# A graph attention layer on one core: aligned parts of V, rows added by GpSimd, late stores, and a first stage with two reductions on GpSimd

## The reference

```python
h = jnp.maximum(_layernorm(x, axis=-1), 0.0)              # x: 4096 x 128, float32
# in the layer, with node_features = h:
h = node_features @ W.T + b_W                              # W: 128 x 128
a1, a2 = (a_vec[:D_OUT], a_vec[D_OUT:])
e = (h @ a1)[:, None] + (h @ a2)[None, :] + b_a[0]         # 4096 x 4096
e = jnp.where(e > 0, e, 0.2 * e)
scores = jnp.where(adjacency_matrix > 0, e, -9e15)         # adjacency: int32, 4096 x 4096
attention = jax.nn.softmax(scores, axis=1)
return x + attention @ h
```

## Time and profile before

| | |
|---|---|
| median of 3 runs | 204.99 us (204.95 to 205.09) |
| profiled execution, its own time | 206.4 us |
| its span, first to last instruction | 204.8 us |
| PE busy | 200.0 us (98%), 3183 matmul instructions |
| PEld busy | 193.5 us (94%) |
| DVE busy | 183.8 us (90%) |
| ACT busy | 142.1 us (69%) |
| POOL busy | 43.7 us (21%) |
| DMA | 75.66 MB, mean 369 GB/s |

### The profile page before, as it was taken

One profiled execution on the slowest core, in us unless ns is written; L12 is line 12 of the kernel. 1 busy time (PEld: TensorE's weight loads), 2 busy tenths in 40 slices (PEclk: granted clock), 3 DMA queues, 4 the chain that ended last, 5 costly groups with the idle time before them and its releaser, 6 DMA issues.

```text
span 204.8 us, 7172 instructions
## 1 busy us (share of the span) xinstructions
PE 200.0 (98%) x3183; PEld 193.5 (94%) x3183; DVE 183.8 (90%) x271; ACT 142.1 (69%) x129; POOL 43.7 (21%) x60
## 2 busy tenths in 40 slices
PE   7989999999999999999999999999999999999994
PEld 7558888999999999999999999999999999999993
DVE  4679999899999799997999998979999899889854
ACT  2289977699770777789777756798777767966000
POOL 1000669699996011070000000000000000000000
PEclk9999999999999999999999999999999999999999
DMA  5999999999999999999999999999999999960312
GB/s 180 366 417 415 405 406 429 413 406 369 429 429 414 418 421 421 416 422 416 413 419 424 402 416 427 422 419 426 414 419 403 406 426 418 426 278 14 104 44 64
DMA packets 15968, 75.66 MB, mean 369 GB/s; under 512 B 1600, under 2 KB 5952, under 8 KB 7616
## 3 DMA queue, kind: packets, MB, share of 16 engines
q1 hardware_dynamic: 15792, 75.06, 90.1%
q10 hardware_dynamic: 144, 0.13, 0.3%
HBM read 73.08 MB, written 2.11 MB: 367 GB/s over the span
## 4 chain that ended last, share of the span: by engine, by line
PE 97%; ACT 1%; issue 0%; DVE 0%; POOL 0%; POOLq 0%
PE ps L834 30%; PE ps L832 28%; PE ps L838 28%; PE ps L806 4%; PE ps L796 3%; PE ps L848 2%; ACT L409 1%; PE ps L874 1%; ACT hT L335 0%; PE ps L852 0%; PE ps L857 0%; DVE xT L539 0%; PE ps L851 0%; DVE rg L512 0%; POOL ones L715 0%
## 5 line engine op out<-in xcount | busy, mean ns | idle before, releaser
L832 PE MATMUL ps<-V,w 128*128 128x129 f16 x1024 | 177.2, 220 | 0.0
L834 PE MATMUL ps<-V,w 128*128 128x129 f16 x1024 | 177.2, 223 | 0.0
L838 PE MATMUL ps<-V,w 128*128 128x129 f16 x1024 | 177.2, 219 | 0.0
L377 ACT ACTIVATE mask<-adj_sb 128x2048 bf16<-128x2048 int32 x63 | 119.6, 1914 | 35.2 <-DMA adj_sb<-in_adj_t 32.4
L457 DVE SCALAR_TENSOR_TENSOR w<-g_row,pairs,mask 128x1024 f32<-128x1024 f32 x96 | 117.7, 1285 | 7.4 <-ACT mask L377 5.0
L838 PEld LDWEIGHTS ps<-V,w 128*128 128x128 f16 x1024 | 102.0, 100 | 0.0
L834 PEld LDWEIGHTS ps<-V,w 128*128 128x128 f16 x1024 | 99.7, 97 | 1.0 <-issue 1.0
L832 PEld LDWEIGHTS ps<-V,w 128*128 128x128 f16 x1024 | 99.2, 97 | 1.5 <-ACT H L340 0.7
L457 DVE SCALAR_TENSOR_TENSOR w<-ps,pairs,mask 128x1024 f32<-128x1024 f32 x31 | 37.5, 1268 | 0.7 <-ACT mask L377 0.7
L786 POOL PARTITION_ALL_REDUCE bad<-bad x1 | 0.4, 380 | 111.3 <-DVE bad L530 111.3
L806 PEld LDWEIGHTS ps<-wp,hT 128*128 128x128 f32 x64 | 8.1, 198 | 2.3 <-ACT hT L335 1.7
(11 more groups left out here) (93 smaller groups left out, 64.6 us busy)
## 6 DMA issues: line engine op xcount, KB each, us to landing
adj_sb<-in_adj_t SPq DMA_DIRECT2D x64, 1024.0 KB, 10.5
xT<-in_x_t SPq DMA_DIRECT2D x8, 256.0 KB, 7.4
x_sb<-in_x_p SPq DMA_DIRECT2D x3, 512.0 KB, 10.8
g_row<-g_dram SPq DMA_DIRECT2D x1, 1536.0 KB, 11.5
out<-xT SPq DMA_DIRECT2D x3, 512.0 KB, 11.4
x_sb<-in_x_p SPq DMA_DIRECT2D x2, 256.0 KB, 4.5
out<-xT SPq DMA_DIRECT2D x1, 192.0 KB, 2.1
out<-xT SPq DMA_DIRECT2D x3, 64.0 KB, 1.5
```

What stands on the lines that cost most here:

```text
L377: nc.scalar.activation(mask[:, m % MASKS, :], adj_sb[:, m % HELD, :], ACT.Relu, scale=CONNECTED).then_inc(mask_ready, 1)
L832: nc.tensor.matmul(sums[:, bank, a, :], w16[:, m % SLOTS, col:col + P, 1], V[:, jt, 0:NF], start=(jt == 0 and a == 0), stop=False, skip_gr ...
L834: nc.tensor.matmul(sums[:, bank, a, :], w16[:, m % SLOTS, col:col + P, 1], V[:, jt, NF:2 * NF], start=False, stop=False, skip_group_check= ...
L838: last = nc.tensor.matmul(sums[:, bank, a, :], w16[:, m % SLOTS, col:col + P, 0], V[:, jt, 0:NF], start=False, stop=(jt == NT - 1), skip_g ...
```

## The change

It has five parts.

1. `V` gets rows of 2 x 136 fp16 numbers instead of 258, and each part uses the first 129 of its 136. Each part now begins at a multiple of 16 bytes.
2. The rows of groups 0 to 2 are added by POOL instead of DVE, behind its first check reduction. The three stores of these rows stand behind the last `adj` load in SP's list instead of between the loads.
3. `norm` and b's constant are reduced by POOL with `partition_all_reduce`. ACT squares W itself and sums along its rows, POOL takes the maximum and the root (`pow` with one half). PE loses L852 and L857. DVE waits for `root_ready` later in its list than before.
4. The first tile of the first `adj` pair is loaded by a DMA of its own, ahead of the second tile, and DVE makes its mask in two halves. There are 7 warming matmuls, and the first centring stands ahead of W a.
5. `ENDS` is 3 instead of 4, and the last check stands behind the reciprocal of the last piece.

```diff
@@ V, WARM, ENDS
+    VW = DOUT + 8
-    WARM = 8
+    WARM = 7
-    ENDS = 4
+    ENDS = 3
-        V = sb("V", [P, NT, 2 * NF], F16)
+        V = sb("V", [P, NT, 2, VW], F16)
@@ SP
+                sp.dma_start(adj_sb[:, 0, 0:GC], adj_t[0, :, 0:GC]).then_inc(tile_loaded, 16)
                 load_xt(3)
-                load_adj(0)
+                sp.dma_start(adj_sb[:, 0, GC:2 * GC], adj_t[0, :, GC:2 * GC]).then_inc(adj_loaded[0], 16)
...
-                    if group >= 2 and at == STORE_AT:
-                        store(group - 2, GI * (group - 2), GI * (group - 1))
-                store(NG - 2, GI * (NG - 2), GI * (NG - 1))
+                for r in range(NG - 1):
+                    store(r, GI * r, GI * (r + 1))
@@ ACT
-                    act.wait_ge(norm_ready, 1)
-                    nc.scalar.activation(root[:], norm[:], ACT.Sqrt).then_inc(root_ready, 1)
...
+                nc.scalar.activation(wsq[:], wp[:, 0:DIN], ACT.Square, scale=(1.02 * DIN) ** 0.5,
+                                     accum_out=norm[:, 0:1]).then_inc(squares_ready, 1)
@@ DVE, first stage
-                dve.wait_ge(norm_summed, 1)
-                nc.vector.tensor_reduce(norm[:], ps[:, 4, 0:DOUT], AX_X, ALU.max).then_inc(norm_ready, 1)
                 statistics(1)
-                dve.wait_ge(cc_done, 1)
+                dve.wait_ge(cc_done, 2)
...
-                early_mask()
+                early_mask(1)
+
+                dve.wait_ge(root_ready, 1)
+                step_(nc.vector.tensor_scalar(gg[:, 0:1], root[:], 1e-30, None, ALU.max))
+                nc.vector.reciprocal(gg[:, 1:2], gg[:, 0:1]).then_inc(g_ready, 1)
+                dve.wait_ge(g_ready, 1)
+                step_(nc.vector.tensor_scalar(rstd[:, 2, 0:GI], rstd[:, 1, 0:GI], gg[:, 1:2], None, ALU.mult))
                 pack(0)
                 scale_weights(0)
+                ones_of(0)
...
-                statistics(2, 5, 8)
+                statistics(2, 3, 8)
@@ DVE, later
-                    if past >= 0 and at in ROWS_AT:
-                        add_rows(past, ROWS_AT.index(at))
@@ POOL
+                pool.wait_ge(wp_loaded, 16)
+                nc.gpsimd.tensor_scalar(ba[:, 0:2], wp[:, AV:AV + 2], wp[:, BW:BW + 1], None, ALU.mult).then_inc(cc_done, 1)
+                pool.wait_ge(cc_done, 1)
+                nc.gpsimd.partition_all_reduce(ba[:, 2:4], ba[:, 0:2], P, RADD).then_inc(cc_done, 1)
+                pool.wait_ge(squares_ready, 1)
+                nc.gpsimd.partition_all_reduce(norm[:, 1:2], norm[:, 0:1], P, RMAX).then_inc(norm_ready, 1)
+                pool.wait_ge(norm_ready, 1)
+                nc.gpsimd.tensor_tensor(root[:], norm[:, 1:2], half_col[:], ALU.pow).then_inc(root_ready, 1)
                 deviations(2, 3)
...
+                for r in range(2 * (NG - 1)):
+                    k = slice(GI // 2 * r, GI // 2 * (r + 1))
+                    pool.wait_ge(scaled_rows, r + 1)
+                    nc.gpsimd.tensor_tensor(Z[:, k, :], Z[:, k, :], x_sb[:, k, :], ALU.add).then_inc(rows_added, 1)
@@ PE
-                nc.tensor.matmul(ps[:, 6, 0:2], wp[:, BW:BW + 1].to_broadcast([P, P]), wp[:, AV:AV + 2], start=True,
-                                 stop=True).then_inc(cc_done, 1)
-                pe.wait_ge(squares_ready, 1)
-                nc.tensor.matmul(ps[:, 4, 0:DOUT], ones[:], wsq[:], start=True, stop=True).then_inc(norm_summed, 1)
```

More of the change, by code:

```diff
@@ L15 @@
 RMAX = bass.bass_isa.ReduceOp.max
+RADD = bass.bass_isa.ReduceOp.add
 LN_EPS = 1e-5
@@ L306, in store @@
                 def store(r, first, last):
-                    sp.wait_ge(rows_ready, 2 * r + 2 if r < NG - 1 else r + NG)
+                    if r < NG - 1:
+                        sp.wait_ge(rows_added, 2 * r + 2)
+                    else:
+                        sp.wait_ge(rows_ready, r - NG + 2)
                     sp.dma_start(out_v[:, first:last, :], Z[:, first:last, :]).then_inc(stored, 16)
                 for m in range(4, NM):
-                    group, at = divmod(m, PAIRS)
                     load_adj(m)
@@ L469, in weigh_first, with early_mask @@
                                                    ALU.min).then_inc(w_begun if half == 0 else w_ready, 1)
-                def early_mask():
-                    dve.wait_ge(adj_loaded[0], 16)
-                    nc.vector.tensor_scalar(mask[:, 0, 0:GC], adj_sb[:, 0, 0:GC], CONNECTED, 0.0, ALU.mult,
+                def early_mask(half):
+                    r = slice(half * GC // 2, (half + 1) * GC // 2)
+                    dve.wait_ge(tile_loaded, 16)
+                    nc.vector.tensor_scalar(mask[:, 0, r], adj_sb[:, 0, r], CONNECTED, 0.0, ALU.mult,
                                             ALU.max).then_inc(mask_early, 1)
@@ L489, in inverse_sums @@
                                             ALU.mult).then_inc(rg_ready, 1)
[L491 to L495, removed]
                 def inverse_last(i):
@@ L510, in inverse_last @@
                         nc.vector.tensor_copy(den[:, r], of).then_inc(den_ready, 1)
+                    else:
+                        check_last()
                     dve.wait_ge(rden_ready, NG - 1 + i + 1)
@@ L567, in scores, with ones_of @@
                                             ALU.mult).then_inc(scores_ready, 1)
+                    if part > 0:
+                        ones_of(part)
+                def ones_of(part):
+                    r = slice(*PARTS[part])
                     nc.vector.reciprocal(H[:, r, ONE], rstd[:, 2, r]).then_inc(ones_ready, 1)
@@ L631, in _ @@
                 nc.vector.reciprocal(rstd[:, 1, 0:GI], rstd[:, 0, 0:GI]).then_inc(std_ready, 1)
-                dve.wait_ge(root_ready, 1)
-                step_(nc.vector.tensor_scalar(gg[:, 0:1], root[:], 1e-30, None, ALU.max))
-                nc.vector.reciprocal(gg[:, 1:2], gg[:, 0:1]).then_inc(g_ready, 1)
-                dve.wait_ge(g_ready, 1)
+                statistics(2, 0, 3)
                 dve.wait_ge(std_ready, 2)
-                step_(nc.vector.tensor_scalar(rstd[:, 2, 0:GI], rstd[:, 1, 0:GI], gg[:, 1:2], None, ALU.mult))
-                statistics(2, 0, 3)
                 scores(0)
@@ L642, in _ @@
                 nc.vector.tensor_reduce(tt[:, 0:1], st[:, 0:GI, T], AX_X, ALU.max).then_inc(t_limits, 1)
-                statistics(2, 3, 5)
+                early_mask(0)
                 dve.wait_ge(t_spread, 1)
```

45 lines of the change are left out of this document (23 added, 22 removed).

## The result

The changed kernel has a median of 221.07 us in four runs (218.51 to 224.66) beside 205.04 for the kernel before; the ratio is 1.074 [1.064, 1.084]. The comparison leaves the run of 224.66 out as disturbed; the other three have a median of 220.46. The profiled execution took 218.51 us with a span of 216.9, so 12.1 us of span more than before.

What follows compares the result with a forecast made beforehand. PE was taken as the bound, 3072 matmuls back to back from the first product. Late root +11.7, clock +2.0, alignment -3.6, step 7 +0.3, end +0.3 make +10.7 us on 204.99: 215.7 us, range 200 to 220.5.

Steps and rivals of the forecast that it cites:

- POOL's code: POOL's first stage: each change between plain operations and reductions costs about 9.1 us of issue; root_ready at 25.9 us.
- The first ISA row: POOL, ahead of the first small product: between 0 and 9.1 us, taken at half, 4.6, for little DMA load.
- The 6 us of the page: Skill page's cost for the first call of freshly loaded POOL code; at 6 us each, root_ready 21.1, time 211.
- Clock and the way to the first product: From root_ready: 0.6 for DVE, 0.8 for pack, 2.7 on PE, 2.0 for PE's clock falling while idle.
- Ends 0 and 4: Range in us given for the loss by PE's lower clock around the first product; 2.0 was taken.
- Alignment: PE's product matmuls: aligned V rids L834 of its excess, gain 3.6 us by durations, 2.8 by chain shares.
- an odd multiple of two bytes: Supposed cause of L834's 223 ns median against 220 and 219: where its read of V's low part starts.
- rival B: Product matmuls: L834's excess belongs to the weights, so aligning V brings nothing; 219.3 us, chance 0.12.
- Rows and stores at 0: Row additions moved to POOL and stores moved behind the loads gain nothing, as PE waits for neither; 0 us.
- Step 7: Products, where DVE's lead is narrowest: PE will wait there for about 0.3 us (0 to 1).
- The end: Behind the last matmuls: with ENDS 3, DVE's closing work and checks add 0.3 us (-0.1 to 0.5).
- Rival A: POOL's code change is short or hidden: 201.3 us, chance 0.28; root_ready costs nothing up to 14.1 us.

Runs made afterwards that it cites:

- par_only: The changed kernel with both reductions on POOL, but b's product and the root made by ACT; 202.82 us, ratio 0.988 to the kernel before.
- hidden_reload: The kernel before with one unused partition_all_reduce added at the head of POOL's list; 205.14 us, ratio 1.001.
- pool_norm_only: The kernel before with part 3 of the change alone (norm and b's constant reduced by POOL); 225.75 us, ratio 1.101.
- product_on_act: The changed kernel with only b's small product moved to ACT, reductions and root staying on POOL; 208.42 us, ratio 1.015 to the kernel before.
- v_aligned: The kernel before with V's rows of 2 x 136 numbers alone; 204.49 us, ratio 0.997.
- aligned_rows_late: The kernel before with parts 1 and 2 (V's rows of 2 x 136, rows added by POOL, late stores); 202.40 us, ratio 0.987.
- after_pe_norm: The changed kernel with both small reductions back on PE, DVE's wait for the root staying late; 202.86 us, ratio 0.989 to the kernel before.
- best_ends4: par_only with ENDS back at 4; 202.36 us, ratio 0.987 to the kernel before.
- v_even4: The kernel before with V in rows of 2 x 130 numbers, low part at byte 260; 204.38 us, ratio 0.997.
- v_high_odd: The kernel before with V's rows of 2 x 136 and the high part begun at byte 2; 204.25 us, ratio 0.995.
- v_swapped: The kernel before with V's two parts swapped in its rows of 258 numbers; 205.64 us, ratio 1.003.

## Why the prediction was right, and where its sizes were off

The mechanism is the one forecast, and the direction is right. The median of 221.07 is 5.4 us above the 215.7 and 0.6 beyond the range of 200 to 220.5; the 220.46 of the other three runs is 4.8 us above and just within it.

- **POOL's code.** "I read 9.1 us as the price of changing POOL's code" held: every such stretch of issue in the traces takes 6.9 to 10.7 us. Two steps were off in opposite ways. The first ISA row, taken at half for the slack DMA engines, took 9.13; the second took 6.90 instead of 9.1, the third 8.53. `root_ready` came at 27.67, 1.8 us late; that it is so near is luck, 4.5 us too little in one step and 2.8 too much in the two others. The first stretch also covers POOL's wait for `wp`, which ACT had by 4.67 us, so it is the least sure of the three. The rule behind it was cruder than the runs show: an ISA row ahead of a reduction that follows the fills costs nothing (par_only, hidden_reload). The 6 us of the page ("GPSIMD Engine Reference" of the Trainium skill, section 2.1) was below every stretch seen.
- **Clock and the way to the first product.** From `root_ready` to there I had 0.6 + 0.8 + 2.7 + 2.0 = 6.1; it took 5.52, and 5.95 and 6.05 in pool_norm_only and product_on_act. In par_only, where nothing waits for POOL, it is 16.57 - 12.21 = 4.36 from `gg` on: the clock cost 1.2 to 1.7 us. "Ends 0 and 4" held.
- **Alignment.** Predicted -3.6, measured -3.0. The shares of the chain had given 2.8 us, and I took the durations instead; the number that I left was the nearer one. From its start to the next one L834 went from 60.7 to 57.0 ns, but the other two lines rose by 0.4 ns each: 2.9 ns for three, times 1024. The cause, "an odd multiple of two bytes", was wrong, and rival B's, the weights, too: what counts is whether a matmul reads on right behind where the one ahead of it stopped.
- **Rows and stores at 0.** Wrong in the other direction: "PE does not wait for loads" was true of slower products, and of the 1.5 MB of stores only 1.0 MB stood between the loads. Without part 2, alignment yields 0.6 us, with it 2.7 (medians of v_aligned and aligned_rows_late).
- **Step 7.** I expected a wait of 0.3 us; the changed kernel has none there, nor have after_pe_norm, par_only and best_ends4, whose first product comes early. I did not look for what gave DVE the time.
- **The end.** +0.2 for +0.3.
- **From span to median.** These terms miss the profiled span by 1.4 us (215.5 to 216.9). The other 4 us are in the medians: the changed kernel's is 2.6 above its profiled execution, the old one's 1.4 below. The latter has a cause that I had noted as a difference and not followed. In the profiled execution of before, the matmuls of L796 ran slow for longer than usual, and the first product came 1.8 us later than in most traces. In before:

```profile
5.55 2.06 PE L796 MATMUL ps<-xT,centre 128*128 128x512 f32 x2
...
7.83 1.92 PE L796 MATMUL ps<-xT,centre 128*128 128x512 f32 x2
...
11.55 1.02 PE L796 MATMUL ps<-xT,centre 128*128 128x512 f32 x2
```

and in v_even4, with the same first stage:

```profile
5.51 1.41 PE L797 MATMUL ps<-xT,centre 128*128 128x512 f32 x2
6.97 1.02 PE L797 MATMUL ps<-xT,centre 128*128 128x512 f32 x2
...
16.52 0.23 PE L833 MATMUL ps<-V,w 128*128 128x129 f16 x1
```

The first product is at 18.31 us there and at 16.52 here. It is the clock, although read 1.00 for the first 10 us: the views show 1.00 where a trace holds no record of the clock, and before's first record, of the upper level, begins at 9.99 us. In v_even4 it begins at 6.14. The 14 traces fall into two lots: first record at 9.2 to 10.8 us (before, aligned_rows_late, v_high_odd, v_swapped), or at 4.4 to 6.2 us (the ten others). In all of them this line's matmuls take 1.06 to 1.20 us each where they end ahead of that record, and 0.59 to 0.70 right behind it. PE had been at work since 1.2 us in all of them. What decides between the two stays open. In one series 4 of 29 runs of the kernel before took 206.2 to 206.6 us, the others 204.5 to 205.3; aligned_rows_late has two levels as well (202.1 to 202.5, and 203.5 and 203.8, the profiled one among the latter). So my base of 18.31 was the rarer start. Why the changed kernel's runs spread over 3 us stays open; the stretches of issue alone, 6.9 to 10.7 us, could do it, but the timed runs have no trace.

Rival A had its point of decision right: with `root_ready` at 8.9 us (par_only) the time is 202.82, where A said 201.3. Its 0.7 us from a shorter first stage didn't come.

## What to carry to other kernels

Count the changes of kind in GpSimd's list, not its operations: put reductions over partitions together, first in the list, and let a change lie where GpSimd waits anyway; a 0.3 us operation of the other kind can cost 12 us. When the bound engine is made faster, ask which engine and which stream stand 2 us behind it, and relieve these too, or the gain is lost there. And look at how the profiled execution lies among the timed ones before its parts are taken as the base; for the clock of the first microseconds, go by the durations of equal matmuls and not by a reading of 1.00.

## What the runs showed of the hardware that I had not expected

- After fills, `partition_all_reduce` starts at once (0.25 us after the start of the last fill), while a `TENSOR_SCALAR` in the same place comes after 9.1 to 10.0 us of issue. From reduction to elementwise it is 7.6 to 10.7 us, from elementwise to reduction 6.9 and 8.8.
- A matmul whose moving operand begins 0 or 2 bytes behind the end of the one ahead's takes 60.3 to 60.8 ns from its start to the next start, the others 56 to 57.
- PE's clock rises at one of two times in the same kernel. In four of the 14 traces the first record of the upper level begins at 9.2 to 10.8 us, in ten at 4.4 to 6.2; with the same first stage (before and v_even4) the first product comes 1.8 us later for it.
